# Cross-attention over 32 sequences: packed score products, two PSUM banks for Q, and block copies of Q issued by SyncE

## What is computed

```
qh = _split_heads(q @ wq.T + bq, h)
kh = _split_heads(k @ wk.T + bk, h)
vh = _split_heads(v @ wv.T + bv, h)
scores = einsum('ntd,nsd->nts', qh, kh) / sqrt(depth)
scores = scores + km * PAD                 # masked keys
attn = softmax(scores, axis=-1)
ctx = einsum('nts,nsd->ntd', attn, vh)
out = _merge_heads(ctx, h) + q
out = (out - mu) / sqrt(var + LN_EPS) * gamma + beta
```

## Time and profile before

| | us |
|---|---|
| median of 3 runs | 1154.09 (1153.67 to 1157.71) |
| the profiled execution: its own time | 1157.28 |
| the profiled execution: span of the records | 1155.5 |
| PE busy | 1123.1 (97%) |
| DVE busy | 822.1 (71%) |
| POOL busy | 771.8 (67%) |
| ACT busy | 612.5 (53%) |

### The profile page before, as it was taken

The page is one execution under the profiler, slowest core; times in us unless marked ns, Lnnn a source line. Parts: engine busy times, 40 slices in busy tenths (PEclk is TensorE's granted clock), DMA queues, the critical chain, the costliest instruction groups (busy, mean ns, idle before and its releaser), DMA issues.

```text
span 1155.5 us, 25702 instructions
## 1 busy us (share of the span) xinstructions
PE 1123.1 (97%) x7541; PEld 1037.8 (90%) x7541; DVE 822.1 (71%) x1622; ACT 612.5 (53%) x1008; POOL 771.8 (67%) x667
## 2 busy tenths in 40 slices
PE   7899999999999999999999999999999999999994
PEld 7788789999999999999999999999999999999983
DVE  5776467777777777777777777777777777777786
ACT  3321254556566555555555656655555555565551
POOL 4999523677766676766667776667676666777465
PEclk9999999999999999999999999999999999999996
DMA  7745433233343444343344333344443334333223
GB/s 228 261 147 188 150 104 90 74 122 95 116 119 117 126 126 126 116 120 99 102 123 122 106 105 119 117 126 126 126 116 122 98 102 123 123 101 110 85 82 128
DMA packets 147207, 141.07 MB, mean 122 GB/s; under 512 B 86452, under 2 KB 88004, under 8 KB 147172
## 3 DMA queue, kind: packets, MB, share of 16 engines
q1 hardware_dynamic: 146564, 140.29, 40.1%
q10 hardware_dynamic: 608, 0.33, 0.1%
HBM read 91.71 MB, written 48.85 MB: 122 GB/s over the span
## 4 chain that ended last, share of the span: by engine, by line
PE 84%; DVE 2%; POOL 1%; issue 0%; ACT 0%; DMA 0%; DVEq 0%; SPq 0%; POOLq 0%
PE q_ps L724 31%; PE o_ps L765 23%; PE s_ps L740 18%; PE t_ps L751 12%; POOL x_lo L991 0%; DVE stats L822 0%; DVE attn L853 0%; PE q_ps L765 0%; DVE y L862 0%; DMA xT_raw<-in_xT 0%; DVE attn L814 0%; DVE row_max L885 0%; DVE y L868 0%; ACT q_hi L1030 0%; DVE y L843 0%
## 5 line engine op out<-in xcount | busy, mean ns | idle before, releaser
L765 PE MATMUL o_ps<-v_tiles,pt 128*128 128x66 f32 x2520 | 310.7, 270 | 1.5 <-DVE attn L814 1.5
L765 PEld LDWEIGHTS o_ps<-v_tiles,pt 128*128 128x128 f32 x2520 | 304.0, 192 | 1.9 <-issue 1.9
L885 DVE TENSOR_REDUCE row_max<-s_ps 128x8 f32<-128x616 f32 x256 | 203.2, 794 | 118.2 <-PE s_ps L740 118.1
L740 PE MATMUL s_ps<-bd,q_hi 128*128 128x308 f32 x1024 | 260.5, 305 | 1.1 <-ACT q_hi L1030 1.1
L991 POOL TENSOR_TENSOR x_lo<-xT_raw,x_hi 128x512 fp32r<-128x512 f32 x124 | 159.3, 1286 | 117.8 <-ACT x_hi L1026 117.7
L961 POOL TENSOR_TENSOR attn<-attn,x_rows 128x512 f32<-128x512 f32 x124 | 160.2, 1292 | 115.8 <-DVE attn L814 115.8
L1036 ACT COPY pt<-t_ps 128x512 f32<-128x512 f32 (+1 forms) x320 | 175.0, 588 | 107.1 <-PE t_ps L751 107.0
L1030 ACT ACTIVATE q_hi<-q_ps,bq_col 128x512 fp32r<-128x512 f32 x125 | 86.1, 689 | 254.9 <-PE q_ps L724 254.9
L724 PE MATMUL q_ps<-x_lo,wq_hi 128*128 128x512 f32 x500 | 218.7, 437 | 2.5 <-PEq L142 2.1
L1016 ACT ACTIVATE probs<-probs 128x616 f32<-128x616 f32 x256 | 183.3, 716 | 64.3 <-DVE probs L894 64.3
L894 DVE TENSOR_TENSOR probs<-s_ps,row_max 128x616 f32<-128x616 f32 x256 | 204.6, 799 | 5.7
(11 more groups left out here) (96 smaller groups left out, 1292.9 us busy)
## 6 DMA issues: line engine op xcount, KB each, us to landing
xT_raw<-in_xT SPq DMA_DIRECT2D x128, 256.0 KB, 3.5
x_rows<-in_x SPq DMA_DIRECT2D x32, 1024.0 KB, 5.6
out<-y SPq DMA_DIRECT2D x128, 256.0 KB, 2.1
k_scratch<-k_out SPq DMA_DIRECT2D x8, 1232.0 KB, 5.4
bd<-k_scratch SPq DMA_DIRECT2D x128, 77.0 KB, 2.4
v_scratch<-v_out SPq DMA_DIRECT2D x16, 264.0 KB
v_tiles<-v_scratch SPq DMA_DIRECT2D x256, 9.9 KB
ctx_raw<-in_ctxT SPq DMA_DIRECT2D x3, 1232.0 KB, 6.2
```

The costliest lines, as they stand in the source:

```text
L740: mm = pe.matmul(s_ps[t % 2][:, j, 0:GS], (q_hi, q_lo)[u][:, g, P * t:P * t + P], bd[par][:, v, g, :, :].rearrange("p h s -> p (h s)"), st ...
L765: mm = pe.matmul(bank_of(b, t)[:, col:col + tile_cols[i]], pt[h][0:w, i, P * t:P * t + P], v_tiles[v_buffer(b, h)][0:w, i, 0:tile_cols[i]] ...
L885: dve.tensor_reduce(row_max[:, u, :].rearrange("p (j h) -> p j h", j=2), score_heads(t), AX.X, ALU.max).then_inc(max_ready, 1)
```

## The change

**Scores.** The three products of a group become three packed ones with fewer columns. `q_a` holds on 96 partitions the high part of heads 0 to 2 and on the last 32 a copy of head 0's high part; `q_c` the low part of heads 0 to 2 and a copy of head 1's high part; `q_b` has head 3 (a copy of its high part, its low part, and its high part again) and head 2's high part. The keys are laid out to match (`k_ac` of 3·78 = 234 columns, `k_b` of 2·78 = 156). So a group's products have 234, 234 and 156 columns in place of three times 308. A head's slot is 78 columns wide with 77 in use. The keys of a sequence need 12 transfers of 32 by 4 by 77 in place of 4 of 32 by 8 by 77.

**Copies between partitions.** Engines write Q where it was computed; the three copies onto other partitions (32 partitions, 128 KB each) are DMA transfers in the list of SP (`move_q`, one for each half of each sequence). `scores` waits for them (`q_moved`). In SP's list half 1 of a stands behind the rows of x of a-1, and half 0 of a+1 behind V of a.

**Q.** `high_q` and `q_low` are two instructions each (96 and 64, 96 and 32 partitions) and stand in other places of their engines' rows; Q has two banks and runs one step earlier against the scores (`q_of_step`). `t_ps` has one bank, and the turns are spread over the steps: `TURNS_AHEAD` before the scores, `TURNS_BEHIND` behind them. The fourth part of x is split in step 7 (`X_STEPS`), and ACT normalises in other steps. Gamma and beta are loaded at the start of phase two. Phase one has small reorderings on ACT and the same split of Q.

```diff
-    GS = HG * S
+    GS = HG * (S + 1)
-    KDMA = HG * DMA
+    KDMA = 3 * HG * DMA
+    QDMA = 3 * DMA
+    SW = S + 1
+    QW = 3 * DH
...
-            t_ps = [ps(two, f"t_ps{i}", [P, BANK]) for i in range(2)]
-            q_ps = ps(two, "q_ps", [P, BANK])
+            t_ps = ps(two, "t_ps", [P, BANK])
+            q_ps = [ps(two, f"q_ps{i}", [P, BANK]) for i in range(2)]
+            X_STEPS = (3, 4, 5, 7)
-            TURNS = ([], [0, 1], [2, 3], [4])
+            TURNS_AHEAD = ([], [1], [], [])
+            TURNS_BEHIND = ([0], [2], [3], [4])
...
+            def q_of_step(s):
+
+                half, u = (s + 1) // 4, (s + 1) % 4
+                return (half + 1) // 2, (0 if half == 1 else 2) + u // 2, u % 2
 
...
-                    for q in range(HG):
-                        rows = slice(DH * q, DH * q + DH)
-                        sp.dma_start(bd[par][rows, :, :, q, :].bitcast(F32), k_dram[b, rows, :, :, :]
+                        sp.wait_ge(zeros_set, 5)
+                    for ac in range(2):
+                        for h in range(3):
+                            rows = slice(DH * h, DH * h + DH)
+                            sp.dma_start(k_ac[par][rows, ac, :, h, 0:S].bitcast(F32), k_dram[b, rows, 0, :, :]
+                                         ).then_inc(k_loaded[par], DMA)
+                        rows = slice(DH * ac, DH * ac + DH)
+                        sp.dma_start(k_ac[par][QW:P, ac, :, ac, 0:S].bitcast(F32), k_dram[b, rows, 1, :, :]
                                      ).then_inc(k_loaded[par], DMA)
+                    for q in range(2):
+                        sp.dma_start(k_b[par][DH * q:DH * q + DH, :, 1, 0:S].bitcast(F32), k_dram[b, QW:P, 0, :, :]
+                                     ).then_inc(k_loaded[par], DMA)
+                        rows = slice(DH * (q + 2), DH * (q + 2) + DH)
+                        sp.dma_start(k_b[par][rows, :, q, 0:S].bitcast(F32), k_dram[b, rows, 1, :, :]
+                                     ).then_inc(k_loaded[par], DMA)
+
+                sp.dma_start(gamma_all[:], gamma.partition_broadcast(P)).then_inc(scale_loaded, DMA)
+                sp.dma_start(beta_all[:], beta.partition_broadcast(P)).then_inc(scale_loaded, DMA)
+
+                def move_q(b, h):
+
+                    sp.wait_ge(q_hi_ready, b * 8 + (4 * h + 4))
+                    g = slice(2 * h, 2 * h + 2)
+                    sp.dma_start(q_a[QW:P, g, :].bitcast(F32), q_a[0:DH, g, :].bitcast(F32)).then_inc(q_moved[h], DMA)
+                    sp.dma_start(q_c[QW:P, g, :].bitcast(F32), q_a[DH:2 * DH, g, :].bitcast(F32)
+                                  ).then_inc(q_moved[h], DMA)
+                    sp.dma_start(q_b[0:DH, g, :].bitcast(F32), q_b[QW:P, g, :].bitcast(F32)).then_inc(q_moved[h], DMA)
...
+                    if real(a):
+                        move_q(a, 1)
...
+                    if real(a + 1) and not in_phase_one(a + 1):
+                        move_q(a + 1, 0)
                     if real(a - 2):
                         store(a - 2, 0, par)
                     if real(a - 2):
...
-                        used = b * 4 + g
-                        if isinstance(used, int) and used <= 4:
-                            used -= 1
-                        at_least(pe, q_hi_ready, used)
-                        at_least(pe, q_lo_ready, used)
+                        at_least(pe, q_hi_ready, b * 8 + (2 * g - 2))
+                        at_least(pe, q_lo_ready, b * 8 + (2 * g - 2))
...
                 def scores(b, h, t, par):
 
-                    pe.wait_ge(q_hi_ready, b * 4 + (2 * h + 2))
-                    pe.wait_ge(q_lo_ready, b * 4 + (2 * h + 2))
+                    pe.wait_ge(q_hi_ready, b * 8 + (4 * h + 4))
+                    pe.wait_ge(q_lo_ready, b * 8 + (4 * h + 4))
+                    pe.wait_ge(q_moved[h], (b + 1) * QDMA)
                     pe.wait_ge(k_loaded[par], b * (KDMA // 2) + (KDMA - par * (KDMA // 2)))
 
                     at_least(pe, shifted, b * 8 + (4 * h + t - 1))
                     for j in range(2):
                         g = 2 * h + j
-                        for n, (u, v) in enumerate(terms):
-                            mm = pe.matmul(s_ps[t % 2][:, j, 0:GS], (q_hi, q_lo)[u][:, g, P * t:P * t + P],
-                                           bd[par][:, v, g, :, :].rearrange("p h s -> p (h s)"),
-                                           start=(n == 0), stop=(n == 2))
+                        for ac, q in ((0, q_a), (1, q_c)):
+                            pe.matmul(s_ps[t % 2][:, j, 0:3 * SW], q[:, g, P * t:P * t + P],
+                                      k_ac[par][:, ac, g, :, :].rearrange("p h s -> p (h s)"),
+                                      start=(ac == 0), stop=False, skip_group_check=True)
+                        mm = pe.matmul(s_ps[t % 2][:, j, 2 * SW:GS], q_b[:, g, P * t:P * t + P],
+                                       k_b[par][:, g, :, :].rearrange("p h s -> p (h s)"),
+                                       start=False, stop=True, skip_group_check=True)
                     mm.then_inc(scores_done, 1)
...
-                    at_least(pe, pt_ready, b * (2 * NT) + (NT * h + i - 1))
+                    at_least(pe, pt_ready, b * (2 * NT) + (NT * h + i))
...
-                        qb = a + h
-                        g = (2 if h == 0 else 0) + t // 2
-                        if real(qb) and not in_phase_one(qb, g):
-                            q_half(qb, g, t % 2, (par + h) % 2)
+                        ahead, g, part = q_of_step(s)
+                        if real(a + ahead) and not in_phase_one(a + ahead, g):
+                            q_half(a + ahead, g, part, (par + ahead) % 2)
+                        last_turns = is_last(a - 1) and h == 0
+                        if last_turns:
+
+                            product(a - 1, h, t)
+                        if real(a - 1 + h):
+                            for i in TURNS_AHEAD[t]:
+                                turn(a - 1 + h, 1 - h, i)
                         if real(a):
                             scores(a, h, t, par)
-                        last_turns = is_last(a - 1) and h == 0
-                        if last_turns:
-
-                            product(a - 1, h, t)
                         if real(a - 1 + h):
-                            for i in TURNS[t]:
+                            for i in TURNS_BEHIND[t]:
...
                 def q_low(b, g):
 
-                    dve.wait_ge(q_hi_ready, b * 4 + (g + 1))
-                    dve.scalar_tensor_tensor(out=q_lo[:, g, :], in0=q_bank(b, g)[:, :], scalar=bq_col[:, g:g + 1],
-                                             in1=q_hi[:, g, :], op0=ALU.add, op1=ALU.subtract
+                    dve.wait_ge(q_hi_ready, b * 8 + (2 * g + 2))
+                    dve.scalar_tensor_tensor(out=q_c[0:QW, g, :], in0=q_bank(b, g)[0:QW, :], scalar=bq_col[0:QW, g:g + 1],
+                                             in1=q_a[0:QW, g, :], op0=ALU.add, op1=ALU.subtract
                                              ).then_inc(q_lo_ready, 1)
+                    dve.scalar_tensor_tensor(out=q_b[DH:2 * DH, g, :], in0=q_bank(b, g)[QW:P, :],
+                                             scalar=bq_col[QW:P, g:g + 1], in1=q_b[QW:P, g, :],
+                                             op0=ALU.add, op1=ALU.subtract).then_inc(q_lo_ready, 1)
...
-                        if 3 <= s <= 6 and real(a + 2):
-                            split_x(a + 2, s - 3, par)
+                        if s in X_STEPS and real(a + 2):
+                            split_x(a + 2, X_STEPS.index(s), par)
...
                 def high_q(b, g):
                     act.wait_ge(q_done, b * 4 + (g + 1))
-                    act.activation(q_hi[:, g, :], q_bank(b, g)[:, :], ACT.Identity, bias=bq_col[:, g:g + 1]
+                    act.activation(q_a[0:QW, g, :], q_bank(b, g)[0:QW, :], ACT.Identity, bias=bq_col[0:QW, g:g + 1]
                                    ).then_inc(q_hi_ready, 1)
+                    act.activation(q_b[P // 2:P, g, :], q_bank(b, g)[P // 2:P, :], ACT.Identity,
+                                   bias=bq_col[P // 2:P, g:g + 1]).then_inc(q_hi_ready, 1)
...
-                        if 3 <= s <= 6 and real(a + 2):
-                            high_x(a + 2, s - 3, par)
-                        g = (2 if h == 0 else 0) + t // 2
-                        if t % 2 == 1 and real(a + h) and not in_phase_one(a + h, g):
-                            high_q(a + h, g)
-
                         if s == 0:
                             if real(a - 1):
                                 exponent(a - 1, 1, 3)
                         elif real(a):
                             exponent(a, (s - 1) // 4, (s - 1) % 4)
+                        ahead, g, part = q_of_step(s)
+                        if part == 1 and real(a + ahead) and not in_phase_one(a + ahead, g):
+                            high_q(a + ahead, g)
                         if real(a - 1 + h):
```

(12 more changed lines are left out.)

118 lines of the change are left out of this document (75 added, 43 removed).

## The result

| | us |
|---|---|
| the changed kernel, median of 4 runs | 1535.53 (1533.74 to 1537.66) |
| the kernel before, beside it, median of 4 runs | 1155.89 (1153.67 to 1157.71) |
| ratio of the two, 95% interval | 1.329 (1.325 to 1.332) |
| span of the profiled execution | 1533.9 |

The change makes the kernel a third slower. PE's share falls from 97% to 78% of the span, and one wait stands out.

What follows compares the result with a forecast made beforehand. PE's instructions bound the old kernel; the change makes PE wait 10 us an iteration for half 1's copies. 27 periods longer by 11.2 us, plus edges, add 324 to 1157, less 3 for the median: 1480 us, range 1356 to 1600.

Steps and rivals of the forecast that it cites:

- Scores: PE's six score products of a step take 0.65 us instead of 0.86, saving 1.7 us an iteration.
- The bound by weight loads: On PE's score products: each needs a weight load and costs about 0.107 us, six 0.65; by columns alone 0.58.
- The rival of dear narrow products: PE's products of 234 and 156 columns run at plain f32 pace, 3.2 us for six, about 1750 us; 8%.
- SP's train: SP's issues after POOL's pass: 1.0 us, keys 6.6, x transposed 2.1, V 5.7; rows of x issued 15.4 after it.
- From the issue of the rows of x to PE's scores: Half 1's copies queue behind the 1 MB: third lands 6.8 us after that issue (bounds 3.9 and 9), scores 0.1 later.
- Half 1 on PE, with the slow clock: From the copies' landing to step 7: 9.9 us of PE work plus 2.4 lost at half clock (1.7 to 3.4).
- POOL's pass: It ends 7.9 us after step 7 starts, 3.0 later than now, because the split of x stands in front.
- these count as nothing on the path: The second Q instructions on ACT and DVE, 2.8 and 3.0 us an iteration, fit in spare time and cost nothing.
- PE's share: PE, idle some 10 us in each iteration before half 1's scores, is about 70% busy.
- Period: An iteration becomes a ring of 9.9, 2.4, 7.9 and 22.3 us: 42.5 for 31.3 now, in 27 iterations.
- The copies of half 0: Not late: they land 7.3 us into step 6 and are wanted at 8.7.
- PE's own iteration: PE's work without DMA waits: 31.3 us less 1.7 for scores plus 0.4 for turns waiting on one bank, 30.0.

Runs made afterwards that it cites:

- the best version: three orders, SyncE plus phase one's old ScalarE order, keys ahead of outputs 2 and 3 of a-3, and POOL scaling before splitting x: 1144.2 us.
- keys later: The changed kernel with the 12 key transfers moved in SP's list from its start to behind outputs 2 and 3 of a-3: 1337.2 us.
- no copies: The changed kernel without the copies of Q and the waits for them, target partitions zeroed once at the start: 1262.3 us.
- three orders, SyncE: The changed kernel with keys moved behind a-3's outputs, half 1's copies ahead of the rows of x, fourth x split in step 6: 1256.9 us.

## Why the prediction was right, and where its sizes were off

The forecast was 1480 us, the measured time 1535.5, inside the range, and the mechanism is the predicted one. By its steps:

- **Scores.** 0.65 us a step forecast, 0.63 measured. The bound by weight loads was the right one of the two; products of 234 columns start 0.11 apart. The rival of dear narrow products fell. The 0.53 us estimated from the Trainium skill, "TensorE: Matmul & The Clock Gate", section "Back-to-back issue gap", is 0.10 too low; the warning of the Trainium skill in the same place, that it undercounts small N in a stream with weight loads, holds.
- **SP's train.** First key to the rows of x: 14.4 forecast, 14.16 measured; the keys 6.6 and 6.14. From POOL's pass to the first key 1.0 and 1.22.
- **From the issue of the rows of x to PE's scores.** 6.9 forecast, 7.7 measured in the iteration at 701.54 (scores at 709.22), 7.95 in the next (745.39 to 753.34) and 8.1 on the mean. This is the first term that was too small: the 1 MB itself took 6.2 in the second of the two and 6.3 in the median, where it took 5.6, and each copy landed some 0.5 behind the one before. The forecast named 9 as the upper bound of the landing and then left it out of the range's upper end: keys at 0.83 and the clock alone made the 1600.
- **Half 1 on PE, with the slow clock.** 12.3 forecast, 12.96 measured (709.22 to 722.18). The clock is the second term that was too small: a loss of 3.1 us here and of 3.4 on the mean, which is the forecast's upper bound, where I took 2.4; single iterations lost up to 4.6.
- **POOL's pass.** 7.9 forecast, 7.83 measured. The chain that the forecast adds up held: ScalarE's copy of x ended 3.85 us behind the start of step 7 for 4.0, the split and the two passes took the rest. But a second chain that it left out, DVE's two `q_low` passes in front of the scaling and so POOL's addition, ended at 3.83, by luck at the same moment, so that the sum came out right. The step "these count as nothing on the path" was wrong here: either chain alone holds POOL, and the experiment that moved the split won 1.3 us in the pass, not the 3.0 that the forecast's step gives.
- **PE's share.** "About 70%" forecast, 78% measured. The forecast divided PE's own 30.0 by 42.5 and left out that work at half clock is busy too: 30.6 + 3.4 of 44.3 is 77%.
- **Period.** 42.5 forecast, 44.3 measured: 27 times 1.8 is 48 of the 55 us that were missing. The rest, and more, is phase one, for which I had 3 us and which took 10.7; the edges of the pipeline gave a little back.
- **The copies of half 0** are not late in the changed kernel, as forecast. The experiments made them late by giving the list back its speed: what was covered by a wait of 10 us was 2.7 us short without it.
- **PE's own iteration.** 30.0 us forecast, 30.6 measured where nothing is waited for. So the packing's gain is 0.6 us an iteration for 1.3 expected, and the best version wins 1%. In its timeline the second of two turns starts 1.28 behind the first (704.29 to 705.57) as forecast (0.44 + 0.63 + 0.2), and the rest of the loss stands in steps 3 and 7, which take 3.89 and 3.84 between their starts (710.70 to 714.59, 726.05 to 729.89) for 3.6.

```profile
704.29 0.60 PE L816 MATMUL t_ps<-ident,probs 128*128 128x128 f32 x4
705.57 0.66 PE L816 MATMUL t_ps<-ident,probs 128*128 128x128 f32 x4
```

## What to carry to other kernels

A new wait on a queue's entry is priced by the whole train ahead of that entry, its issues (0.5 us each here), the waits inside it and the bytes in flight ahead of it, not by the transfer; read the queue's own timeline before deciding which engine issues. The same three copies, issued by the same engine, cost 273 us in the changed kernel (against the run without them) and no recurring wait in the last run, where the order of SP's list and of POOL's row is another. A second queue takes them out of the train of issues but not out of the company of the bytes: from ScalarE's queue they still took up to 6 us beside 1 MB of SP's. When a long wait is taken away, count the ring again with everything that it covered: here V of half 1, then the copies of half 0, then a buffer shared with POOL came up one by one.

## What the runs showed of the hardware that I had not expected

A transfer of 128 KB between partitions of the on-chip memory lands in 2.3 to 2.4 us, about as an output tile of 256 KB to DRAM (2.1), and in 5.8 behind 1 MB on its queue. On another queue beside 1 MB it took 6.0.

The price of a stall in clock hardly grew with its length, and did not follow from its length alone. These are the waits of PE in the steady part of four runs, and the loss behind each, read from the granted clock of the 13 us behind it:

| run | wait, us | loss by the clock, us |
|---|---|---|
| the change | 25 of 10.5 (9.8 to 11.4) | 1.7 to 4.6, mean 3.4 |
| keys later | 24 of 4.2 (3.5 to 5.1) | 1.7 to 4.6, mean 3.0 |
| no copies | 24 of 2.3 (1.9 to 2.7) | 1.7 to 3.4, mean 2.0 |
| three orders, SyncE | the last 21 of 25, 2.6 to 2.8 | none |

```profile
719.57:732.00 12.43, 12.39 (x90) 11.38 (x91) 10.05 (x21) 6.59 (x10) 3.38 (x4) 1.00 0.50 142
```

This line is the stretch behind a wait of 2.67 us in the run with three orders: the clock stayed at its full level, while waits as short, without the copies, cost 2 us each. So halving a long wait saved almost nothing in clock, and of short waits some kinds cost two thirds of a long one and others nothing. What decides between them was not tested.
